# The row that one-hots are compared with, laid out as 15 padded runs of 32 (relational graph layer, one core)

## The chip, the core and the metric

The kernel runs on one core of one Trainium2 chip. The metric is the device time of one execution in microseconds, the median of several runs. A core has a matrix engine (PE), a vector engine (DVE), a scalar engine (ACT), GpSimd (POOL), a synchronisation engine (SP) and 16 DMA engines. Each engine works off its own queue in order, and engines meet at semaphores. "PEld" in the profile is the loading of matrix weights, and "POOLq", "SPq" and the like are the sequencers of the engines.

## The reference

There are 6250 nodes with 128 features each (`x`), and 106250 edges sorted by destination `dst`, each with a source `src` and one of 40 types. For each destination node and type the source rows are summed; each sum goes through the matrix of its type; the results, the counts of edges times a feature row per type, a norm by degree, a loop matrix, a ReLU, a residual and a layer norm follow.

```python
seg = edge_dst * 40 + edge_type
S = segment_sum(h[edge_src], seg, 6250 * 40).reshape(n, r, d)
cnt = segment_sum(ones, seg, 6250 * 40).reshape(n, r)
agg = einsum('nrd,rdf->nf', S, relation_weights) + cnt @ rFeatures
h = agg * deg ** -0.5
h = relu(h + h @ loop_weight)
x = layernorm(x + h)
```

## The kernel before

**Tiles.** The edges are cut into tiles of 128 (`P`), 831 of them (`USED`), 17 to a block (`TPB`); there are 49 blocks (`BLOCKS`), one for each 128 destination nodes. The edges of a tile fall on at most 12 neighbouring nodes (`WIN`), so a tile's sums fit a window of 40 types by 12 nodes, 480 columns.

**One tile.** GpSimd gathers the 128 source rows into `rows` (function `gather`, line 442: an indirect DMA from the DRAM table `x_parts`, in which each row of `x` lies as a rounded part and a rest, 1 KB together). DVE builds the one-hot matrix `hot` of 128 edges by 480 columns (`one_hot`, line 727): it compares a row of the numbers 0 to 479 (`iota`, FP16) with each edge's key `key_f`, type times 12 plus the node's place in the window, one number per partition. PE multiplies the 2 parts of the rows by `hot` into one of 7 PSUM banks (line 929, N = 480, twice for a tile), after a small product of 12 columns for the counts (line 922). ACT copies 11 of every 12 columns of the bank into `ring` (line 529), DVE adds the first column, which two tiles can share (line 829). `ring` holds the sums of four blocks.

**One block.** Once a block's tiles are in `ring`, PE multiplies the 41 pieces by the relation weights into `agg_ps` (line 939, spread over the tiles of the two next blocks), and DVE merges the 12 columns that spill into the next block (line 787), clears two stretches (lines 798 and 799, copies of `zeros`), builds two small one-hots for each half block (lines 736 and 739), and runs nine short steps of the norm (lines 750 to 779, among them the TENSOR_SCALARs of lines 758, 768 and 779).

**What sets the order.** Every engine's program is written out by hand. In DVE's step for tile t the one-hot of tile t + 7 (`AHEAD`; `hot` has 8 buffers) stands ahead of the add of tile t, which waits for ACT's copy of tile t. PE starts a pair of tiles t, t + 1 when DVE has added tile t - 6 (that frees the bank of tile t + 1). GpSimd issues the gather of tile t when PE has done tile t - 17 (`tile_done`; `rows` has 17 places).

**The first five blocks** (85 tiles, `PLAIN`) gather from `x` itself into `raw` (line 448), and ACT and DVE split these rows into the two parts (lines 505 and 723), while SP, ACT and DVE write the table `x_parts` in ten stages (lines 383, 498, 716 and 405). The gather of tile 85, the first of line 442, waits for the table, and for tile 68 to be done.

Of the kernel before, what the change touches and what calls it, by code (L numbers as in the profile page):

```python
# [5 lines left out]
ALU = mybir.AluOpType  # L6
# [3 lines left out]
FP16 = mybir.dt.float16  # L10
# [3 lines left out]
P = 128  # L14
N, E, D, R = 6250, 106250, 128, 40
# [12 lines left out]
WIN = 12  # L28
# [3 lines left out]
AHEAD = 7  # L32
COLS_T = TILES + TPB
POS = 20
POS_LOAD = 4
ROUND_SHIFT = 10
ROUND_MULT = -(-(1 << ROUND_SHIFT) // SEGS)
# [74 lines left out]
def build(nc, x, src_main, src_rest, dst_main, dst_rest, type_main, type_rest, r_features, relation_w, loop_w, out):  # L112
    with ExitStack() as ctx:
        x_parts = nc.dram_tensor("x_parts", [N, PARTS * D], F32, kind="Internal").ap()

        def sb(name, shape, dt):
            return ctx.enter_context(nc.sbuf_tensor(name, shape, dt))
# [4 lines left out]
        def sem(name):  # L122
            return ctx.enter_context(nc.semaphore(name))
# [9 lines left out]
        key_f = sb("key_f", [P, COLS_T], F32)  # L133
        pos = sb("pos", [1, BLOCKS * POS], I32)
        iota = sb("iota", [P, R * WIN], FP16)


        ring = sb("ring", [P, COLS, SEGS * SEG], F32)
# [9 lines left out]
        def pieces_in(flat):  # L148
# [8 lines left out]
        head, head_next, head_seg, head_off, head_gap, blk_i, rounds, pos_2d = (  # L157
            piece(POS)[0:BLOCKS].bitcast(I32) for _ in range(8))
        after = piece(TILES)
        iota_i = piece(R * WIN).bitcast(I32)  # L160
# [18 lines left out]
        hot = sb("hot", [P, HOTS, R * WIN], F32R)  # L179
# [77 lines left out]
        hot_ready = sem("hot_ready")  # L257
# [34 lines left out]
        def clear_ring(copy, segs):  # L292

            for s in segs:
                copy(ring[:, :, s * SEG:s * SEG + WIN], zeros[:])
                ins = copy(ring[:, :, s * SEG + BLOCK:(s + 1) * SEG], zeros[:])
            ins.then_inc(ring_zero, 1)
# [28 lines left out]
        def window(eng, regs, i, k):  # L326

            if k % POS_LOAD == 0:
                n = min(POS_LOAD, TPB - k)
                at = i * POS + k  # L330
                eng.load(regs[k:k + n], pos[0:1, at:at + n] if isinstance(i, int) else pos[0:1, bass.ds(at, n)])
# [20 lines left out]
        def column(t):  # L352
            return slice(t, t + 1) if isinstance(t, int) else bass.ds(t, 1)
# [15 lines left out]
        def _(sp):  # L369
# [20 lines left out]
            sp.wait_ge(pos_done, 1)  # L390
            sp.dma_start(pos[:].rearrange("o (b k) -> o b k", k=POS)[:, :, 0:TPB], pos_2d[:, 0:TPB]).then_inc(pos_ready, 16)
            w_v = relation_w.rearrange("r d f -> d r f")
# [23 lines left out]
        def _(pool):  # L416
# [8 lines left out]
            nc.gpsimd.iota(iota_i, pattern=[[1, R * WIN]], base=0, channel_multiplier=0)  # L425
            nc.gpsimd.iota(blk_i, pattern=[[0, POS]], base=0, channel_multiplier=1).then_inc(iota_done, 1)
            pool.wait_ge(const_done, 1)
# [216 lines left out]
        def _(dve):  # L644
# [9 lines left out]
            nc.vector.memset(hot_type[:, :, R:], 0.0).then_inc(types_padded, 1)  # L654
            dve.wait_ge(iota_done, 1)
            nc.vector.tensor_copy(iota[:], iota_i)
            dve.wait_ge(zeros_done, 1)
            clear_ring(nc.vector.tensor_copy, CLEARS[0])

# [64 lines left out]

            def one_hot(t, buffer):

                nc.vector.tensor_scalar(hot[:, buffer], iota[:], key_f[:, column(t)], None, ALU.is_equal).then_inc(  # L727
                    hot_ready, 1)

            def one_hot_types(i, h):  # L730

# [69 lines left out]
            def step(i, tiles, sums, late, fin):  # L801
                c = i - 3
                for k in range(TPB):
                    if sums and known(i, 2) and k == SAFE:
                        merge(i, tiles)
                    if tiles and k < tiles_of(i):
                        t = i * TPB + k
                        if k % 2 == 0:
                            ahead, j = pair_ahead(i, k, LOW_AHEAD)
                            if isinstance(ahead, int) and ahead < PLAIN_BLOCKS:  # L810
                                low(ahead, j)
                        if k == 4:
                            one_hot_types(i, 1)
                        if k == 14 and known_less(i, LAST):
                            clear(i)
                        if k == 13 and known_less(i, LAST):
                            one_hot_types(i + 1, 0)
                        if known_less(t + AHEAD, USED):
                            one_hot(t + AHEAD, (t + AHEAD) % HOTS)
                        if isinstance(i, int) and k in STAGE_AT.get(i, ()):  # L820
                            stage_low_part(stage_of(i, k))
                        start = window(dve, regs, i, k)

                        dve.wait_ge(copied, t + 1)
                        at_least(dve, added, t)
                        if k == 0 and known(i, 1):
                            dve.wait_ge(cleared, i)
                        a = ring[:, :, bass.ds(start, 1)]
                        nc.vector.tensor_tensor(a, a, win_ps[bank_of(t)][:, :, 0:1], ALU.add).then_inc(added, 1)  # L829
                    if fin:  # L830
                        finish(c, k)
# [9 lines left out]
            def in_order():  # L841
                one_hot_types(0, 0)
                for t in range(AHEAD):
                    one_hot(t, t % HOTS)
                for n in range(STAGED_FIRST):
                    stage_low_part(n)
                for j in range(LOW_AHEAD):
                    low(0, j)
                dve.wait_ge(pos_ready, 16)
                dve.wait_ge(ring_zero, len(CLEARS))  # L850
                run(dve, step)
                drain()
# [234 lines left out]
```

## Time and profile before

| | us |
|---|---|
| median of 3 runs | 1139.66 (1138.44 to 1141.38) |
| the profiled execution, its own time | 1136.47 |
| its span, first to last instruction | 1134.7 |

| engine | busy us | share of the span |
|---|---|---|
| PE | 978.5 | 86% |
| PEld | 863.6 | 76% |
| POOL | 822.3 | 72% |
| DVE | 749.0 | 66% |
| ACT | 525.5 | 46% |

Busy time is an average over stages that have different limits; what bounds a stage is read from which wait ends last in it. Records of DVE instructions overlap by up to 0.1 us, so that the busy time of an engine is less than the sum of its instructions' durations. A timeline row gives the start, the duration, the engine, the line of the code, what is written and read, and in brackets how long the engine had been idle and what released it.

### The profile page before, as it was taken

What the parts mean: (1) busy time and instruction counts of PE and PEld (TensorE: products, weight loads), DVE (VectorE), ACT (ScalarE), POOL (GpSimd) and SP (SyncE); (2) the same over time, 40 slices, a digit from 0 to 9 for tenths busy, and PEclk for the clock granted to TensorE, in tenths of its full rate; (3) what the DMA queues carried; (4) which work ended last, traced back from release to release, by engine and by line L of the source; (5) the groups of instructions that cost most, each with busy time, mean ns of one, the idle gap of its engine ahead of it and who ended that gap; (6) DMA issues with size and microseconds to landing.
All of it is one profiled execution on the core that took longest, in us unless ns stands there. A gap on an engine that the chain in (4) does not pass through costs nothing.

```text
span 1134.7 us, 25029 instructions
## 1 busy us (share of the span) xinstructions
PE 978.5 (86%) x6713; PEld 863.6 (76%) x6713; DVE 749.0 (66%) x2585; ACT 525.5 (46%) x1134; POOL 822.3 (72%) x846
## 2 busy tenths in 40 slices
PE   2345999998999999989899999989989999998997
PEld 1224999987887787888788878778878878877887
DVE  6344887777666666767766766666666666666663
ACT  2234765544444444445444444444444444444441
POOL 7773467777777777777777777777777777777770
PEclk9556999999999999999999999999999999999999
DMA  6543133333333333333333333333333333333330
GB/s 163 177 162 140 41 87 106 106 110 111 111 108 110 110 108 110 110 108 112 106 110 108 114 111 106 111 111 107 111 109 108 109 109 110 108 110 107 111 108 28
DMA packets 61567, 124.92 MB, mean 110 GB/s; under 512 B 15540, under 2 KB 33338, under 8 KB 61422
## 3 DMA queue, kind: packets, MB, share of 16 engines
q0 software_dynamic: 38512, 103.28, 31.6%
q1 hardware_dynamic: 8878, 13.65, 3.5%
q10 hardware_dynamic: 14032, 6.35, 2.0%
q8 instruction: 55, 0.90, 0.3%
q14 instruction: 90, 0.74, 0.2%
HBM read 113.62 MB, written 9.60 MB: 109 GB/s over the span
## 4 chain that ended last, share of the span: by engine, by line
PE 43%; DMA 33%; POOL 14%; issue 6%; DVE 2%; SPq 1%; ACT 1%; POOLq 0%; ACTq 0%; DVEq 0%
DMA rows<-x_parts,src 27%; PE win_ps L929 22%; PE agg_ps L939 18%; POOL rows L442 14%; DMA x_in<-x 6%; PE win_ps L1016 1%; PE win_ps L965 1%; DVE x_out L716 1%; ACT x_out L498 1%; PE win_ps L922 1%; SPq L397 0%; DMA w<-type_rest 0%; PE win_ps L902 0%; PE win_ps L964 0%; POOLq L441 0%
## 5 line engine op out<-in xcount | busy, mean ns | idle before, releaser
L442 POOL DMA_INDIRECT rows<-x_parts,src x746 | 734.5, 985 | 243.7 <-issue 121.9
L529 ACT COPY ring<-win_ps 128x451 f32 x831 | 464.3, 559 | 515.3 <-PE win_ps L929 503.0
L929 PE MATMUL win_ps<-hot,rows 128*128 128x480 f32 x1662 | 580.0, 434 | 83.8 <-DMA rows<-x_parts,src 71.8
L939 PEld LDWEIGHTS agg_ps<-ring,w 128*128 128x128 f32 x3936 | 553.5, 191 | 48.0 <-DVE ring L829 6.7
L939 PE MATMUL agg_ps<-ring,w 128*128 128x128 f32 x3936 | 561.8, 275 | 6.1 <-DVE ring L829 6.1
L727 DVE TENSOR_SCALAR hot<-iota,key_f 128x480 fp32r<-128x480 f16 x831 | 401.5, 484 | 0.3 <-issue 0.2
L829 DVE TENSOR_TENSOR ring<-ring,win_ps 128x41 f32 x831 | 188.4, 227 | 311.7 <-ACT ring L529 307.4
L929 PEld LDWEIGHTS win_ps<-hot,rows 128*128 128x128 f32 x1662 | 258.5, 194 | 138.9 <-DMA rows<-x_parts,src 124.9
L922 PEld LDWEIGHTS win_ps<-hot_node,hot_type 128*128 128x128 bf16 x831 | 81.6, 100 | 58.5 <-DVE hot_type L739 29.6
L922 PE MATMUL win_ps<-hot_node,hot_type 128*128 128x12 bf16 x831 | 85.8, 170 | 45.7 <-DVE hot_type L739 24.7
L448 POOL DMA_INDIRECT raw<-x,src x85 | 86.0, 1011 | 42.0 <-issue 22.6
L739 DVE TENSOR_TENSOR hot_type<-iota,typ_f 128x320 bf16<-128x320 f16 x98 | 49.5, 506 | 0.1
L716 DVE TENSOR_TENSOR x_out<-x_in,x_out 125x640 fp32r<-125x640 f32 x10 | 8.2, 824 | 50.0 <-ACT x_out L498 50.0
L498 ACT CAST x_out<-x_in 125x640 fp32r<-125x640 f32 x10 | 7.2, 724 | 67.9 <-DMA x_in<-x 54.6
L787 DVE TENSOR_TENSOR ring<-ring 128x492 f32<-128x492 f32 x48 | 31.7, 661 | 0.0
L799 DVE COPY ring<-zeros 128x492 f32<-128x492 f32 x48 | 31.4, 654 | 0.0
L798 DVE COPY ring<-zeros 128x492 f32<-128x492 f32 x48 | 31.0, 646 | 0.0
L736 DVE TENSOR_TENSOR hot_node<-iota,rel_f 128x96 bf16<-128x96 f16 x98 | 25.1, 256 | 0.4 <-issue 0.4
L965 PE MATMUL win_ps<-loop,agg_sb 128*128 128x128 f32 x96 | 22.4, 316 | 0.0
L964 PEld LDWEIGHTS win_ps<-ones,cnt_sb 128*128 128x128 f32 x96 | 18.0, 188 | 2.8
L505 ACT CAST rows<-raw 128x256 fp32r<-128x256 f32 (+1 forms) x45 | 17.5, 394 | 1.3 <-DVE out_sb L779 1.2
L723 DVE TENSOR_TENSOR rows<-raw,rows 128x256 fp32r<-128x256 f32 (+1 forms) x45 | 17.9, 403 | 0.2 <-ACT rows L505 0.2
(85 smaller groups left out, 247.2 us busy)
## 6 DMA issues: line engine op xcount, KB each, us to landing
rows<-x_parts,src POOLq DMA_INDIRECT x746
x_parts<-x_out SPq DMA_DIRECT2D x10, 625.0 KB
x_in<-x SPq DMA_DIRECT2D x10, 312.5 KB
out<-out_sb ACTq DMA_DIRECT2D x48, 64.0 KB
x_blk<-x ACTq DMA_DIRECT2D x47, 64.0 KB
w<-relation_w SPq DMA_DIRECT2D x8, 320.0 KB
raw<-x,src POOLq DMA_INDIRECT x85
w<-dst_main SPq DMA_DIRECT2D x1, 415.0 KB
```

The lines of the kernel that those rows point to most:

```text
L442: pool.indirect_dma_start(rows[0:n, k].rearrange("p c d -> p (c d)").bitcast(F32), None, x_parts, bass.IndirectOffsetOnAxis(ap=src[0:n, t: ...
L448: pool.indirect_dma_start(raw[:, t % RAW], None, x, bass.IndirectOffsetOnAxis(ap=src[:, t:t + 1], axis=0)).then_inc(gathered[k], 16)
L529: nc.scalar.copy(ring[:, :, bass.ds(start + 1, WIN - 1)], win_ps[bank_of(t)][:, :, 1:WIN]).then_inc(copied, 1)
L727: nc.vector.tensor_scalar(hot[:, buffer], iota[:], key_f[:, column(t)], None, ALU.is_equal).then_inc(hot_ready, 1)
L739: nc.vector.tensor_tensor(hot_type[:, at, 0:R], iota[:, 0:R].unsqueeze(1).to_broadcast([P, n, R]), typ_f[:, ts].unsqueeze(2).to_broadcast( ...
L787: nc.vector.tensor_tensor(ring[:, :, bass.ds(head, WIN)], ring[:, :, bass.ds(head, WIN)], ring[:, :, bass.ds(tail + BLOCK, WIN)], ALU.add) ...
L799: nc.vector.tensor_copy(ring[:, :, bass.ds(old + BLOCK, WIN)], zeros[:]).then_inc(cleared, 1)
L829: nc.vector.tensor_tensor(a, a, win_ps[bank_of(t)][:, :, 0:1], ALU.add).then_inc(added, 1)
L922: nc.tensor.matmul(banks[bank_of(n)][:, R * WIN:COLS * WIN], hot_type[:, n % TPB], hot_node[:, n % TPB], start=True, stop=True)
L929: ins = nc.tensor.matmul(banks[bank_of(t)][:, 0:R * WIN], rows[:, k, part, :], hot[:, t % HOTS], start=False, stop=(part == PARTS - 1), sk ...
L939: ins = nc.tensor.matmul(agg_ps[:], w[:, r, :], ring[:, r, bass.ds(seg, BLOCK)], start=(r == 0), stop=(r == COLS - 1))
L965: nc.tensor.matmul(ps[:, 0:D], agg_sb[:], loop[:], start=True, stop=True).then_inc(fin_done, 1)
```

## The change

A second row of the numbers 0 to 479, `iota_rows`, is made once at the start: 15 runs of 32 numbers with one pad element behind each, so that a run begins every 33 elements. The one-hot of a tile reads this row in place of `iota`. The numbers compared, the key, the result and its place are the same. `iota` stays, for the small one-hots.

```diff
+HOT_ROWS = 15
+HOT_RUN = R * WIN // HOT_ROWS
+assert HOT_ROWS % 2 and HOT_ROWS * HOT_RUN == R * WIN
...
         iota = sb("iota", [P, R * WIN], FP16)
+        iota_rows = sb("iota_rows", [P, HOT_ROWS, HOT_RUN + 1], FP16)
...
             nc.vector.tensor_copy(iota[:], iota_i)
+            nc.vector.tensor_copy(iota_rows[:, :, 0:HOT_RUN], iota_i.rearrange("p (a b) -> p a b", a=HOT_ROWS))
...
             def one_hot(t, buffer):
 
-                nc.vector.tensor_scalar(hot[:, buffer], iota[:], key_f[:, column(t)], None, ALU.is_equal).then_inc(
-                    hot_ready, 1)
+                nc.vector.tensor_scalar(hot[:, buffer].rearrange("p (a b) -> p a b", a=HOT_ROWS), iota_rows[:, :, 0:HOT_RUN],
+                                        key_f[:, column(t)], None, ALU.is_equal).then_inc(hot_ready, 1)
```

In the built program the order of DVE's instructions is the same but for one more cast. These are its rows at the start of the program, before; each names the line, the operation, what is written and read, and the form that is written (`w` is the buffer in which the whole numbers lie at that time; lines 295 and 296 clear `ring`):

```order
L656 CAST iota<-w 128x480
L295 COPY ring<-zeros 128x41x12
L296 COPY ring<-zeros 128x41x12
L661 CAST typ_f<-w 128x850
L662 CAST dst_f<-w 128x850
```

And now (the lines of the code stand four or five further down):

```order
L660 CAST iota<-w 128x480
L661 CAST iota_rows<-w 128x15x32
L299 COPY ring<-zeros 128x41x12
L300 COPY ring<-zeros 128x41x12
L666 CAST typ_f<-w 128x850
L667 CAST dst_f<-w 128x850
```

The cast into `iota_rows` is new and writes 15 runs of 32; nothing else moved. Further on DVE, where the tiles begin, the rows before are:

```order
L739 TENSOR_TENSOR hot_type<-iota,typ_f 128x8x40
L727 TENSOR_SCALAR hot<-iota,key_f 128x480 x7
L716 TENSOR_TENSOR x_out<-x_in,x_out 125x5x128
L723 TENSOR_TENSOR rows<-raw,rows 128x2x128 x4
L727 TENSOR_SCALAR hot<-iota,key_f 128x480
```

And now:

```order
L744 TENSOR_TENSOR hot_type<-iota,typ_f 128x8x40
L732 TENSOR_SCALAR hot<-iota_rows,key_f 128x480 x7
L721 TENSOR_TENSOR x_out<-x_in,x_out 125x5x128
L728 TENSOR_TENSOR rows<-raw,rows 128x2x128 x4
L732 TENSOR_SCALAR hot<-iota_rows,key_f 128x480
```

The one-hots stand where they stood. They read `iota_rows`, and the written form is still one run of 480: the program merges the 15 runs of `hot`, which touch, while those of `iota_rows` do not touch and stay apart.

## Rows read from the trace of the kernel before

**Rows 1.** The page: the chain that ended last, by engine.

```profile
PE 43%; DMA 33%; POOL 14%; issue 6%; DVE 2%; SPq 1%; ACT 1%; POOLq 0%; ACTq 0%; DVEq 0%
```

**Rows 2.** Timeline, POOL: start us, us, instruction, idle time and releaser.

```profile
147.09 0.97 POOL L442 DMA_INDIRECT rows<-x_parts,src  x1 [16.76 <-PE win_ps L929]
...
154.89 0.95 POOL L442 DMA_INDIRECT rows<-x_parts,src  x1 [0.30 <-issue]
...
1107.64 0.89 POOL L442 DMA_INDIRECT rows<-x_parts,src  x1 [0.30 <-issue]
```

**Rows 3.** Line 442 by itself: count, duration ns min/median/max, first and last start.

```profile
L442 POOL DMA_INDIRECT rows<-x_parts,src x746: 887/946/1357, 147.1 to 1107.6; - x187
```

**Rows 4.** The page, costliest groups: count, busy us, mean ns, idle before.

```profile
L442 POOL DMA_INDIRECT rows<-x_parts,src x746 | 734.5, 985 | 243.7 <-issue 121.9
...
L727 DVE TENSOR_SCALAR hot<-iota,key_f 128x480 fp32r<-128x480 f16 x831 | 401.5, 484 | 0.3 <-issue 0.2
L829 DVE TENSOR_TENSOR ring<-ring,win_ps 128x41 f32 x831 | 188.4, 227 | 311.7 <-ACT ring L529 307.4
```

**Rows 5.** Two stretches: busy us (count) of PE, PEld, DVE, ACT, POOL; clock, DMA.

```profile
108.00:147.00 39.00, 38.68 (x280) 36.23 (x281) 35.49 (x121) 28.61 (x66) 17.45 (x17) 0.96 0.17 52
...
228.00:1107.00 879.00, 798.52 (x5519) 705.35 (x5518) 591.05 (x2050) 414.71 (x886) 670.76 (x684) 1.00 0.38 109
```

**Rows 6.** These and the one between, DVE's one-hots of line 727 alone.

```profile
108.00:147.00 39.00, 17.41 (x37) 0.96 0.17 52
147.00:228.00 81.00, 36.22 (x76) 1.00 0.37 106
228.00:1107.00 879.00, 330.77 (x681) 1.00 0.38 109
```

**Rows 7.** Single lines of DVE: count, duration ns min/median/max, first and last start.

```profile
L727 DVE TENSOR_SCALAR hot<-iota,key_f x831: 448/464/702, 20.1 to 1103.0; 128x480 fp32r<-128x480 f16 x167
...
L758 DVE TENSOR_SCALAR h_sb<-fin_sb,norm x48: 274/277/515, 137.9 to 1121.7; 128x128 f32<-128x128 f32 x48
...
L787 DVE TENSOR_TENSOR ring<-ring x48: 656/660/672, 121.0 to 1112.5; 128x492 f32<-128x492 f32 x48
...
L799 DVE COPY ring<-zeros x48: 645/654/661, 67.0 to 1090.6; 128x492 f32<-128x492 f32 x48
```

**Rows 8.** Groups of DVE, each shape apart: count, busy us, mean ns.

```profile
L762 DVE TENSOR_TENSOR y_sb<-h_sb,x_blk 128x128 f32<-128x128 f32 x49 | 13.8, 282 | 0.1
```

**Rows 9.** Timeline of POOL beside DVE, at three places.

```profile
362.36 1.13 POOL L442 DMA_INDIRECT rows<-x_parts,src  x1 [0.30 <-issue]
362.59 0.46 DVE L727 TENSOR_SCALAR hot<-iota,key_f 128x480 fp32r<-128x480 f16 x1
...
367.69 0.95 POOL L442 DMA_INDIRECT rows<-x_parts,src  x1 [0.30 <-issue]
367.94 0.66 DVE L799 COPY ring<-zeros 128x492 f32<-128x492 f32 x1
...
498.96 0.95 POOL L442 DMA_INDIRECT rows<-x_parts,src  x1 [0.30 <-PE win_ps L929]
499.49 0.65 DVE L727 TENSOR_SCALAR hot<-iota,key_f 128x480 fp32r<-128x480 f16 x1
```

**Rows 10.** Timeline of DVE (adds of tiles 29 and 62, early work) and of SP.

```profile
107.48 0.22 DVE L829 TENSOR_TENSOR ring<-ring,win_ps 128x41 f32 x1
...
141.79 0.22 DVE L829 TENSOR_TENSOR ring<-ring,win_ps 128x41 f32 x1
...
6.22 0.71 DVE L661 CAST typ_f<-w 128x850 f32<-128x850 int32 x1 [2.42 <-DMA w<-type_rest]
...
22.80 0.82 DVE L716 TENSOR_TENSOR x_out<-x_in,x_out 125x640 fp32r<-125x640 f32 x1
...
27.87 0.43 SPq L383 DMA_DIRECT2D x_in<-x  x1
```

**Rows 11.** Timeline of PE: the start of the pair of tiles 68 and 69.

```profile
145.55 0.20 PE L922 MATMUL win_ps<-hot_node,hot_type 128*128 128x12 bf16 x2
```

## The prediction

> **What bounds the kernel now.** I read the page first, then the timeline of each engine. The page alone misleads: PE is busy for 86% of the span and POOL for 72% (the table above), and the chain that ended last is mostly PE and DMA [rows 1]. But POOL never waits in the long stage. The first gather of line 442 starts at 147.09 us, after a real wait of 16.76 us, and the last at 1107.64 [rows 2]. In between each of the 745 steps is one gather and then about 0.30 us idle, whichever releaser stands beside that idle time (the page has "issue" and PE); the pause is the same everywhere, so it belongs to the gather. The check: a gather takes 985 ns in the mean [rows 4], and (1107.64 - 147.09) / 745 = 1289 ns, so the pause is 304 ns. POOL is saturated for 960 us though it counts as busy for three quarters of them.
>
> The others have room. From 228 to 1107 us, 681 tiles pass at 1291 ns each. DVE works 591.05 / 681 = 868 ns for a tile [rows 5, 6]. PE was busy for 798.52 / 681 = 1173 ns of each; from 147 to 228 us, where its rows lie ready, it did 76 tiles in 81 us, 1066 ns for each, at a granted clock of 1.00 as later on (2.4 GHz) [rows 6]. The 16 DMA engines are busy for 38% [rows 5]. So there are three stages: up to 108 us the table is written, whose loads and stores alternate; to about 228 us PE is the bound, with its rows gathered ahead; from there POOL is, and it has been falling behind since its start at 147.09. The end is POOL's start, plus 746 gathers, plus a tail of 27.1 us behind the start of the last one (1134.7 - 1107.64).
>
> **Why a gather takes longer than it must.** Its median is 946 ns and its mean 985 [rows 3, 4]: most take 946, a part much longer, up to 1357. I laid the start of each gather beside DVE's instructions. 281 gathers have no one-hot running between 150 and 620 ns after their start (the first at 154.89, the last at 1107.64 [rows 2]); they take 945 ns in the mean and 963 at most. The other 465 take 1008. One pair shows it: a one-hot that starts 0.23 us after the gather makes it 1.13 us [rows 9]. It goes the other way too: where the gather is already in the middle of its work the one-hot pays, with 0.65 us in place of 0.46 [rows 9], and its maximum is 702 ns [rows 7]. And it isn't DVE as such: a longer copy of line 799 starts 0.25 us after the gather, and the gather still takes 0.95 [rows 9]. Line 787 and line 799 never leave 645 to 672 ns, while line 758 goes from 277 to 515 [rows 7].
>
> What sets the two kinds apart can be read from durations. Line 758 and the one-hot are both TENSOR_SCALARs with a number per partition: 128 elements in 277 ns, 480 in 464 [rows 7]; the slope is 187 / 352 = 0.53 ns for an element, the fixed part 209 ns. Lines 762 and 787 are both TENSOR_TENSORs: 128 elements in 282 ns [rows 8], 492 in 660 [rows 7]; the slope is 378 / 364 = 1.04 ns. So the one-hot goes at two elements in the time of one, and the kind that goes at double speed is the kind that excludes GpSimd. The copy of line 799 is the useful neighbour: it has one input like a one-hot, but its source is one run of 492 and its target 41 runs of 12. It takes 654 ns, the slow speed. A source and a target with unlike counts of runs, one even and one odd, lose the double speed here. The changed one-hot mirrors that: source 15 runs, target one run of 480.
>
> **The change, part by part.** *The one-hot itself.* At the slow speed it costs 209 + 480 x 1.04 = 709 ns. Bounds: 464 ns at the lower end, if nothing switches; at the upper end line 829, which steps by a whole row for each of its 41 elements and takes 227 ns [rows 4], so with the 149 ns that line 762 has beyond 128 x 1.04 that is (227 - 149) / 41 = 1.9 ns for an element, and a one-hot of 209 + 480 x 1.9 = 1121 ns. I take 709: the source still runs in pieces of 32 neighbours, like line 799's pieces of 12, which cost nothing extra. DVE then spends 709 - 484 = 225 ns more on each tile, 868 + 225 = 1093 ns, below POOL's 1250 and within the kernel's period. Cover: DVE waits for ACT before its adds; the one-hots stand seven tiles ahead, so what they add falls into these waits. It would be gone at 1250 ns.
>
> *The gather.* No long gathers are left: 945 + 304 = 1249 ns in place of 1289. The gain is the term that counts: 745 x 40 = 29.8 us by the starts; by the durations (985 - 946) x 746 = 29.1. I take 29.1. The short TENSOR_SCALARs of lines 758, 768 and 779 keep the fast form, about 132 of them in the stage. Of gathers without a one-hot in their middle, 14 had line 758 there, and none was over 948 ns; so I cost them at zero. Upper bound: as much as a one-hot costs now, 39 ns each, 5 us.
>
> *The start of the gathers.* It hangs on tile 68, and so on PE between 108 and 147 us. There DVE is the fuller engine than later: 35.49 of 39 us for 37 tiles [rows 5, 6], as it also splits raw rows. PE's pair 68, 69 needs DVE's add of tile 62. Before, DVE went from the add of tile 29 to that of tile 62, 33 steps, in 141.79 - 107.48 = 34.3 us [rows 10], 3.3 of them idle (of the 3.5 that the stretch has). Now 34.3 - 3.3 + 33 x 0.245 = 39.1 (against this stage's undisturbed 464 ns); with one longer one-hot ahead of tile 29's add, it is done at 107.48 + 0.25 + 39.1 + 0.2 = 147.0. PE began that pair at 145.55 [rows 11]. So the first gather starts some 1.5 us later. Behind it DVE needs about 1.2 us for a tile until the split rows end at tile 84, still under 1249, and POOL doesn't wait again. Bounds: nothing, if DVE's idle time was more than I counted; 5 us, if all of 35.49 + 37 x 0.245 - 39 = 5.6 shows.
>
> *The rest.* The added cast, about half a microsecond, lies ahead of the cast of line 661, before which DVE had stood idle for 2.42 us on a load [rows 10]: free; without that cover, 0.5 us. The seven one-hots ahead of the table's first part (line 716) are 1.7 us longer, but DVE was done with that part at 23.6 us and SP only came to the table's next load at 27.9, behind its weight loads [rows 10]: free. In the tail no one-hot is left (the last starts at 1103.0 [rows 7]).
>
> **Sum.** The span: 1134.7 - 29.1 + 1.5 = 1107.1. The profiled execution took 1136.47, 1.8 beyond its span, and the median of the runs shown is 3.2 above that. I carry the difference of 27.6 to the median: 1139.66 - 27.6 = 1112.1 us.
>
> **The rivals.** *Nothing switches.* If the engine keeps two elements at a time, the one-hot takes 464 ns, or 8 rows of 32 at 0.53 x 2 each, 480; the long gathers stay, and the time is 1140. Line 799 speaks against it, but there the odd count is the target's. The Trainium skill, VectorE: DVE Perf Modes, section on Mode 2×_2P, asks for outermost counts in source and destination that are both even, or odd and equal. By that rule one run of 480 gives the slow speed, and 15 runs on both sides would have given this rival; by the built program it is the first, so that the rule comes out at 1112, and line 799 agrees.
>
> *Half the gain.* The switch comes, but a run that begins at an odd element costs something, or the short TENSOR_SCALARs now meet the gathers. Each 0.1 us on a one-hot delays the first gather by 33 x 0.1 = 3.3 us; at 800 ns that is 3 us, with the 5 us of the short ones 8: 1120.
>
> *DVE becomes the bound (slower).* The place is DVE's queue from 228 us on: with a one-hot of H ns it needs 868 + H - 484 for a tile. From H = 866 on that is over POOL's 1250; from 905 on, over today's 1289. At the upper bound, 1121 ns, it is 1505 ns: 746 x 0.216 = 161 us more, with the delayed start some 1315 us. Against it: it takes 1.45 ns for an element, and the rows with runs of neighbours show 1.04 [rows 7, 8]. The Trainium skill, Vector Engine (DVE) Microarchitecture Reference, section 5.2, has one source that hops at every element at 1.73 ns and pairs that begin on an odd word at 1.30 (4-byte words). By its figures, an estimate, the one-hot would be 209 + 480 x 1.30 = 833 ns, still faster than before; only hops at every element would decide for this rival, and here there are 14 hops in 480. No row here shows an odd begin.
>
> **How the numbers follow.** Forecast, 1108 to 1117: 0.72. Half the gain, 1117 to 1130: 0.13. Nothing switches, 1138 to 1142: 0.10. DVE the bound, above 1143: 0.05. About 0.3% is what a measurement of this kernel can tell from no change, 3.4 us. So faster 0.85, same 0.10, slower 0.05. The range takes the forecast's case and the better part of the second: from 1107.5 (a gain of 29.8, no delay, and 2 us of scatter between medians) to 1122.
>
> **What would show it.** The one-hot at 700 to 720 ns with hardly any spread; the gathers of line 442 with a mean within 3 ns of their median of 946; starts 1250 ns apart; the first one at 148 to 149 us; DVE busy for 82 to 87% of the span, its waits for ACT nearly halved; lines 758, 768 and 779 still going up to 0.5 us. Wrong would be: one-hots at 460 to 480 (nothing switched); one-hots near 700 but a mean gather still at 985 (the exclusion has another cause than the speed); a first gather past 152 us (the early stage mis-sized); PE waiting for the one-hots after 228 us (DVE is the bound).

## The result and the profile after

| | before | after |
|---|---|---|
| median, us | 1139.99 (1138.44 to 1141.38, 4 runs) | 1123.00 (1122.10 to 1124.12, 4 runs) |
| ratio | | 0.985 (0.983 to 0.987) |
| span of the profiled execution, us | 1134.7 | 1120.2 |

The change gains 1.5%. The forecast was 1112.1 us with a range up to 1122: the direction was right, the gain was 17 us where 27.6 were expected, and the time lies just above the range. The two profiled executions are 14.5 us apart in span and not 17, since the one before lay 3.5 us below its median and the one after 0.9 below its own.

The page of the changed kernel, its busy time, the chain by engine, and the groups that answer to [rows 4] (one-hot now line 732, gather 446, add 834):

```profile
PE 972.0 (87%) x6713; PEld 861.6 (77%) x6713; DVE 914.3 (82%) x2586; ACT 525.7 (47%) x1134; POOL 806.2 (72%) x846
...
PE 46%; DMA 34%; POOL 9%; issue 6%; DVE 3%; ACT 1%; SPq 1%; DVEq 0%; POOLq 0%; ACTq 0%
...
L446 POOL DMA_INDIRECT rows<-x_parts,src x746 | 719.5, 964 | 245.0 <-PE win_ps L934 139.9
...
L732 DVE TENSOR_SCALAR hot<-iota_rows,key_f 128x480 fp32r<-128x480 f16 x831 | 585.2, 705 | 0.2
...
L834 DVE TENSOR_TENSOR ring<-ring,win_ps 128x41 f32 x831 | 186.7, 225 | 141.5 <-ACT ring L533 135.8
```

Each line by itself (count, duration ns min/median/max), to be read against [rows 3, 7]:

```profile
L732 DVE TENSOR_SCALAR hot<-iota_rows,key_f x831: 691/705/737, 20.4 to 1088.3; 128x480 fp32r<-128x480 f16 x167
```

```profile
L446 POOL DMA_INDIRECT rows<-x_parts,src x746: 942/946/1463, 147.4 to 1092.8; - x187
```

And the timeline of POOL, first and last gather, the counterpart of [rows 2]:

```profile
147.43 0.94 POOL L446 DMA_INDIRECT rows<-x_parts,src  x1 [18.08 <-PE win_ps L934]
...
1092.84 1.04 POOL L446 DMA_INDIRECT rows<-x_parts,src  x1 [0.31 <-issue]
```

The one-hot takes 705 ns, with a spread of 46 ns where it was 254: it went over to one element at a time (709 was worked out for that), and it is no longer stretched beyond 737. POOL is still the bound, its gathers back to back from 147.43 to 1092.84 us. The stream of 745 steps is 945.4 us where it was 960.6. That is 15.1 us less; the start (0.3 us later) and the tail (27.4 us for 27.1) give back 0.6, and the span is 14.5 us shorter. But a gather still takes 964 ns in the mean with a median of 946. The long gathers are fewer, not gone, and the longest is longer than before.

### The profile page after: what moved, and what is told of

Same layout as the page of the kernel before. It is cut to its first block, busy times and chain, and to the rows that moved or that the text cites. A ratio compares the mean times of both kernels' runs of the same rounds, so it can differ in the third digit from the quotient of the medians.

```text
span 1120.2 us, 25030 instructions
## 1 busy us (share of the span) xinstructions
PE 972.0 (87%) x6713; PEld 861.6 (77%) x6713; DVE 914.3 (82%) x2586; ACT 525.7 (47%) x1134; POOL 806.2 (72%) x846
## 4 chain that ended last, share of the span: by engine, by line
PE 46%; DMA 34%; POOL 9%; issue 6%; DVE 3%; ACT 1%; SPq 1%; DVEq 0%; POOLq 0%; ACTq 0%
DMA rows<-x_parts,src 28%; PE win_ps L934 24%; PE agg_ps L944 19%; POOL rows L446 9%; DMA x_in<-x 5%; PE win_ps L1021 1%; PE win_ps L970 1%; PE win_ps L927 1%; DVE x_out L721 1%; SPq L401 1%; ACT x_out L502 0%; DVE hot L732 0%; ACT ring L533 0%; DVE ring L834 0%; DMA w<-type_rest 0%
## 5 line engine op out<-in xcount | busy, mean ns | idle before, releaser
L446 POOL DMA_INDIRECT rows<-x_parts,src x746 | 719.5, 964 | 245.0 <-PE win_ps L934 139.9
L732 DVE TENSOR_SCALAR hot<-iota_rows,key_f 128x480 fp32r<-128x480 f16 x831 | 585.2, 705 | 0.2
L927 PE MATMUL win_ps<-hot_node,hot_type 128*128 128x12 bf16 x831 | 85.8, 170 | 43.8 <-DVE hot_type L744 22.4
L970 PE MATMUL win_ps<-loop,agg_sb 128*128 128x128 f32 x96 | 22.4, 316 | 0.0
```

What stands on the lines that cost most here:

```text
L446: pool.indirect_dma_start(rows[0:n, k].rearrange("p c d -> p (c d)").bitcast(F32), None, x_parts, bass.IndirectOffsetOnAxis(ap=src[0:n, t: ...
L732: nc.vector.tensor_scalar(hot[:, buffer].rearrange("p (a b) -> p a b", a=HOT_ROWS), iota_rows[:, :, 0:HOT_RUN], key_f[:, column(t)], None, ...
L927: nc.tensor.matmul(banks[bank_of(n)][:, R * WIN:COLS * WIN], hot_type[:, n % TPB], hot_node[:, n % TPB], start=True, stop=True)
L970: nc.tensor.matmul(ps[:, 0:D], agg_sb[:], loop[:], start=True, stop=True).then_inc(fin_done, 1)
```

## What holds the long gathers

I took all 746 gathers of the changed kernel against DVE's instructions again. 92 take more than 955 ns. In 83 of them, with 13.7 of the 14.1 us that all have beyond 946 ns, the gather ends 817 ns, to within 20, behind the end of an instruction that reads two inputs from SBUF and, but for three of them, was running when the gather began: the merge of line 792 (24 gathers, 6.6 us), the small one-hots of lines 744 and 741 (42, 5.5 us), and lines 767, 776 and 728 (17, 1.6 us). The timeline of POOL and DVE, a gather held and one not held:

```profile
154.92 0.54 DVE L744 TENSOR_TENSOR hot_type<-iota,typ_f 128x360 bf16<-128x360 f16 x1
154.95 1.33 POOL L446 DMA_INDIRECT rows<-x_parts,src  x1 [0.30 <-PE win_ps L934]
155.36 0.72 DVE L732 TENSOR_SCALAR hot<-iota_rows,key_f 128x480 fp32r<-128x480 f16 x1
...
1026.75 0.95 POOL L446 DMA_INDIRECT rows<-x_parts,src  x1 [0.30 <-PE win_ps L934]
1026.79 0.67 DVE L792 TENSOR_TENSOR ring<-ring 128x492 f32<-128x492 f32 x1
```

Line 744 ends at 155.46, and 155.46 + 0.82 = 156.28 is the end of the gather (154.95 + 1.33). The merge that starts 0.04 us behind its gather doesn't hold it. So a gather needs something at its start that a two-input instruction has taken; an instruction that ends within 946 - 817 = 129 ns of the gather's start costs it nothing. A two-input instruction that begins by itself later in the gather doesn't hold it.

With this in hand, the pair of [rows 9] reads otherwise than I read it. One more row of the kernel before, the instruction ahead of that one-hot, with the two rows again in mind:

```profile
362.01 0.66 DVE L787 TENSOR_TENSOR ring<-ring 128x492 f32<-128x492 f32 x1
```

The merge ends at 362.67; 362.67 + 0.82 = 363.49 is the end of that gather (362.36 + 1.13). The one-hot that I blamed only stood behind the merge.

The fast one-hot does hold gathers, but at two points, and not anywhere in their middle as I had it. Two pairs of the kernel before:

```profile
169.01 0.46 DVE L727 TENSOR_SCALAR hot<-iota,key_f 128x480 fp32r<-128x480 f16 x1
169.22 1.07 POOL L442 DMA_INDIRECT rows<-x_parts,src  x1 [0.30 <-PE win_ps L929]
...
171.85 1.03 POOL L442 DMA_INDIRECT rows<-x_parts,src  x1 [0.30 <-issue]
172.31 0.45 DVE L727 TENSOR_SCALAR hot<-iota,key_f 128x480 fp32r<-128x480 f16 x1
```

The first one-hot is running when its gather begins, and the gather ends 0.82 us behind the one-hot's end (169.47 + 0.82 = 170.29), as behind a two-input instruction. The second begins 0.46 us after its gather, and the gather ends 0.12 us behind the one-hot's end (172.76 + 0.12 = 172.88). Of the 212 gathers over 955 ns of the kernel before, with 29.0 us beyond 946, 106 are of the first kind (16.6 us) and 37 of the second (3.7 us; lags of 116 to 122 ns, one-hots that began 0.38 to 0.63 us after the gather). Another 65 (8.6 us) end 817 ns, to within 20, behind a two-input instruction. Four are left, with under 0.1 us. Where a one-hot began 0.13 to 0.35 us after the gather and nothing at double speed or with two inputs was running at its start (53 gathers), none took over 955 ns. In the changed kernel none of the second kind is left.

The Trainium skill, SBUF — State Buffer, section "Who interferes with whom", says that a DVE instruction with two SBUF inputs contends with a GpSimd instruction that reads SBUF, and one in a two-port mode with GpSimd at large. The trace agrees with both, with the 817 ns above; that a gather reads its row numbers (`src`) from SBUF at its start would fit the first, but no run here shows what it is that the gather needs, nor what it needs the second time.

## The experiments

Each has its gathers' row from the page; the medians are from the line's own view. Mean less median, times 746, is the sum that the long gathers cost; by this measure the kernel before has (985 - 946) x 746 = 29.1 us [rows 3, 4], the changed one 13.4. Each such sum comes from one trace. The kernel before ran beside all of them: 1140.31 us beside e1 to e4 (16 runs), 1140.95 beside e9 to e11 (9 runs).

**e1: an even count of runs.**

```diff
-HOT_ROWS = 15
+HOT_ROWS = 16
```

> The changed kernel with 16 padded runs of 30 in place of 15 of 32; all else is the same. Theory (what decides the one-hot's speed is that the counts of runs of source and target are unlike, one of them odd, and not the pad or the gaps): with 16 runs against one run of 480 both counts are even, the one-hot falls back to about 464 ns at the shortest, with a maximum near 700, and the time to that of the kernel before, 1136 to 1142 us. Rival (a source in padded runs is slow in itself): the one-hot stays at 705 ns and the time at 1123.

1140.29 us, ratio 1.000 (0.998 to 1.002). The one-hot and the gathers:

```profile
L732 DVE TENSOR_SCALAR hot<-iota_rows,key_f x831: 448/462/703, 20.3 to 1109.1; 128x480 fp32r<-128x480 f16 x167
```

```profile
L446 POOL DMA_INDIRECT rows<-x_parts,src x746 | 740.0, 992 | 244.6 <-issue 126.2
```

```profile
L446 POOL DMA_INDIRECT rows<-x_parts,src x746: 942/949/1372, 147.7 to 1113.8; - x187
```

With 16 padded runs the one-hot is fast again, and the whole gain is gone. Pad, gaps and odd begins (16 runs of 30 every 31 elements have them too) cost nothing. What decides is the count of the source's runs, 15 or 16, against a target in one run of 480 elements: the odd count is slow, the even one fast.

This trace has the fast one-hot and the two-input instructions of the kernel before, and its long gathers sum to (992 - 949) x 746 = 32.1 us where that one's sum to 29.1. By holder the difference is larger: 76 gathers with 13.1 us behind two-input instructions (65 with 8.6 there), 156 with 19.9 us behind the one-hot (143 with 20.3). So how much each kind holds differs by some us from one trace to the next, with the same work.

**e2 and e3: more load on DVE, with two inputs and with one.** e2 writes the larger small one-hot once more, e3 copies `zeros` twice more, both into the idle staging buffer.

```diff
+                if i >= 3:
...
+                    nc.vector.tensor_tensor(
+                        spare[:, 0:n * R].rearrange("p (t r) -> p t r", r=R),
+                        iota[0:X_PARTS, 0:R].unsqueeze(1).to_broadcast([X_PARTS, n, R]),
+                        typ_f[0:X_PARTS, ts].unsqueeze(2).to_broadcast([X_PARTS, n, R]), ALU.is_equal).then_inc(extra_done, 1)
```

```diff
+                if i >= 3:
+                    for _ in range(2):
...
+                        nc.vector.tensor_copy(spare[:, 0:COLS * (WIN + 1)].rearrange("p (r n) -> p r n", r=COLS)[:, :, 0:WIN],
+                                              zeros[0:X_PARTS]).then_inc(extra_done, 1)
```

> The changed kernel, and from block 3 on DVE makes the second small one-hot (two inputs in SBUF, 320 or 360 elements, 0.5 us) a second time into a spare buffer, 92 more such instructions. Theory (a gather whose start falls into a DVE instruction with two SBUF inputs waits for its end and then needs about 817 ns): such stretches are longer by 0.44 us twice a block, the sum of what gathers take beyond 946 ns goes from 14.3 us to 25 to 32, and the time from 1123 to 1134 to 1141 us. Rival (the gathers that are still long in the changed kernel come from DVE being busier, or from DMA): 92 x 0.44 = 40 us more of DVE's time in 960 would add 0 to 3 us.

> The changed kernel, and from block 3 on two more copies of zeros (one input, the slow form, 492 elements, 0.65 us) behind the two clears, into a spare buffer, 90 more instructions, some 52 us more of DVE's time: more load than in the run with the small one-hots made twice. Theory (only two SBUF inputs, or the double speed, keep a gather waiting): gathers stay at a mean of 963 to 966 ns, the time stays within 2 us of 1123. Rival (DVE's load makes gathers long): the mean rises to 975 or more, the time by 8 us or more.

e2: 1131.44 us (1130.81 to 1134.03), e3: 1126.82 (1126.18 to 1128.67). The page's gathers of e2, then of e3:

```profile
L447 POOL DMA_INDIRECT rows<-x_parts,src x746 | 728.4, 976 | 245.7 <-PE win_ps L945 137.1
```

```profile
L447 POOL DMA_INDIRECT rows<-x_parts,src x746 | 723.7, 970 | 246.4 <-PE win_ps L944 140.0
```

The order is as expected, the sizes are not: e2 added 8.4 us to the changed kernel's 1123 for 33 us more of DVE's busy time where 11 to 18 were expected, e3 3.8 for 46 us where under 2 were. Both have a median gather of 949 ns and not 946, which is 2.2 us in each; e1 and e10 have it too, and its cause is open. Beyond it e2 has (976 - 949) x 746 = 20.1 us and e3 15.7, against 13.4. So the added two-input instructions cost about three times what the one-input ones cost (6.7 and 2.3 us), with more of DVE's time in the cheaper run. In e3 it is line 747, the small one-hot, that holds more gathers than before (43 with 8.0 us, by the same 817 ns; line 744 of the changed kernel has 37 with 5.2). That the added copies shifted it against the gathers is a guess; the copies themselves held none.

**e4: the merge as a copy.**

```diff
-                nc.vector.tensor_tensor(
-                    ring[:, :, bass.ds(head, WIN)], ring[:, :, bass.ds(head, WIN)],
-                    ring[:, :, bass.ds(tail + BLOCK, WIN)], ALU.add).then_inc(merged, 1)
+                nc.vector.tensor_copy(ring[:, :, bass.ds(head, WIN)], zeros[:]).then_inc(merged, 1)
```

> The changed kernel with the merge (492 elements, two inputs in the ring, 0.66 us) replaced by a copy of zeros of the same size and duration to the same place; this leaves out the sums that cross two blocks. Theory: the merges' share of the long gathers goes, 6.7 of 14.3 us by the trace of the changed kernel, and the time falls from 1123 to 1115 to 1118 us. Rival (the one-hot that follows the merge is what makes the gather long): the copy is followed by the same one-hot, nothing changes, 1123.

1117.04 us (1115.27 to 1118.77), as the theory has it:

```profile
L446 POOL DMA_INDIRECT rows<-x_parts,src x746 | 712.2, 955 | 245.0 <-PE win_ps L932 138.7
```

**e9 and e10: without two-input instructions, behind the slow and the fast one-hot.** The merge as in e4, and from block 3 on:

```diff
+                if i >= 3:
+                    flat = zeros[:].rearrange("p r n -> p (r n)")
...
+                    nc.vector.tensor_copy(
+                        hot_node[:, at].rearrange("p t n -> p (t n)").rearrange("p (a b) -> p a b", a=runs),
+                        flat[:, 0:runs * (run + 1)].rearrange("p (a b) -> p a b", a=runs)[:, :, 0:run])
+                    ts_, cols = (5, 64) if n == 8 else (9, R)
+                    nc.vector.tensor_copy(
+                        hot_type[:, at.start:at.start + ts_, 0:cols],
+                        flat[:, 0:n * R].rearrange("p (a b) -> p a b", a=ts_)).then_inc(types_ready, 1)
+                    return
```

> The kernel of the run without the merge and the small one-hots again (both replaced by copies of zeros, sums across blocks and counts by type left out), for a time on a chip where the gathers are back to back: the last such run had gathers of 947 ns in the mean, but all its engines stopped together 168 times or so, and its time can't be used. Theory (two SBUF inputs at the start of a gather are all that is left): gathers at 947 to 953 ns, the stream of 746 at 934 to 938 us, the time 1109 to 1113 us, ratio to the kernel before 0.973 to 0.977. Rival (another cost of 8 us or more came with the slower one-hot): above 1116.

> The same two replacements in the kernel before, with its fast one-hot (sums across blocks and counts by type left out). Theory (each kind holds up its own gathers): the fast one-hots' share stays, 17 to 22 us of 29; the time is 7 to 12 us below the kernel before, 1128 to 1133. Then the one-hot's share is what the change took away. Rival of my prediction (the one-hots hold up all of the long gathers): no change, 1138 to 1141.

e9: 1111.38 us, ratio 0.975 (0.972 to 0.978). e10: 1130.87 us, ratio 0.991 (0.988 to 0.995). Line 446 of e9 and line 442 of e10, by themselves and on the page:

```profile
L446 POOL DMA_INDIRECT rows<-x_parts,src x746: 880/946/1136, 150.3 to 1083.3; - x187
...
L446 POOL DMA_INDIRECT rows<-x_parts,src x746 | 707.0, 948 | 245.1 <-PE win_ps L944 147.1
```

```profile
L442 POOL DMA_INDIRECT rows<-x_parts,src x746: 887/949/1241, 147.8 to 1104.1; - x187
...
L442 POOL DMA_INDIRECT rows<-x_parts,src x746 | 730.1, 979 | 244.6 <-issue 122.5
```

Both times and both ratios came out as the theories have them. The stream of e9, 1083.3 - 150.3 = 933.0 us, and the fast one-hots' share in e10, 22.4 us, lie just outside what was named (934 to 938, and 17 to 22). Together with the two kernels they make a square:

| long gathers, us (median time, us) | merge and small one-hots as they are | replaced |
|---|---|---|
| fast one-hot | 29.1 (1140.0) | 22.4 (1130.9) |
| slow one-hot | 13.4 (1123.0) | 1.5 (1111.4) |

By these four traces the two causes don't add up: the fast one-hot costs 15.7 us beside the others and 20.9 alone, the others 6.7 beside it and 11.9 alone. With e1's trace in the first cell (32.1 us) it is 18.7 and 20.9, 9.7 and 11.9; by the times it is 17.0 and 19.5, 9.1 and 11.6. That a gather which one cause no longer holds at its start can fall to the other is plausible, but a difference of 2 to 5 us between single traces doesn't show it. What the square shows is that each cause costs time without the other, and that both together are all but 1.5 us of the long gathers.

**e5 to e8: the same questions on another chip.** e5 is the changed kernel once more, e8 is e9's kernel. e7 makes the larger small one-hot in three pieces, in steps of their own; e6 makes the merge in three as well.

```diff
+                        if k == 1:
+                            types_nodes(i, 1)
+                        if k in (2, 3, 4):
+                            types_piece(i, 1, k - 2)
...
+                        if k == 9 and known_less(i, LAST):
+                            types_nodes(i + 1, 0)
+                        if k in (11, 12, 13) and known_less(i, LAST):
+                            types_piece(i + 1, 0, k - 11)
```

> The changed kernel as it is, on the chip of the three runs that follow, so that they can be compared with it there: 1121 to 1127 us by both theories, gathers with a median of 946 to 949 ns, beyond it 13 to 17 us in sum.

> The changed kernel with the same work in pieces: the larger of the small one-hots (360 and 320 elements) in three pieces of 2 or 3 tiles, the merge in three pieces of 13 or 14 relations, each piece in a step of its own with the one-hot of 480 behind it. Theory (a gather that starts inside an instruction with two SBUF inputs, or a chain of such, waits for its end and needs 817 ns from there; so what an instruction costs grows with the square of its length beyond 0.13 us, and a one-hot between two pieces lets the gather in): of the 12 us that merges and small one-hots cost, 2 to 4 stay; the sum of what gathers take beyond their median is 4 to 6 us, the time 8 to 10 us below the changed kernel on this chip, 1113 to 1117. Rival (the sum of such stretches decides, not their length, or the lock goes over to the one-hot that follows): the same 14 us or, with 6 more instructions a block, more; 1122 to 1128.

> Of the run in pieces the small one-hots alone; the merge stays whole. Theory: some 4 to 5 us below the changed kernel on this chip, 1117 to 1121, the merges' 6 to 7 us stay. Rival: no change, 1122 to 1126.

> The changed kernel with the merge and, from block 3 on, both small one-hots replaced by copies of zeros (one input, the slow form, the same number of elements); this leaves out the sums across blocks and the counts of edges by type. Theory: of the long gathers only those beside the norm's steps and the first blocks are left, 1 to 3 us, all gathers at a mean of 947 to 953 ns, and the time is 10 to 13 us below the changed kernel on this chip, 1110 to 1114, which is also what my forecast of 1112 had taken for the changed kernel itself. Rival (something else than two inputs makes them long): above 1118.

On this chip the kernel before took 1388.44 us (29 runs), and these 1396.05, 1402.06, 1394.32 and 1394.25, all far from the 1110 to 1128 us expected. The page of e5, its chain and its gathers:

```profile
PE 57%; another core or an unknown queue 14%; issue 13%; ACT 9%; DMA 3%; DVE 2%; ACTq 2%; SPq 0%; DVEq 0%
...
L446 POOL DMA_INDIRECT rows<-x_parts,src x746 | 719.2, 964 | 482.8 <-PE win_ps L934 202.8
```

The gathers were no longer than elsewhere (964 ns), but POOL stood idle for twice as long (482.8 us), 168 times for more than 0.4 us, and in the one stretch that I followed, at 405 us, PE, ACT and DVE stood idle with it; the granted clock was 0.87 over the whole execution where it was 0.97. What stopped them stays open. There POOL isn't the bound, and the change makes the kernel slower: ratio 1.005 (1.003 to 1.007). The times decide nothing about e6 to e8. Their gathers do: means of 960 (e6), 959 (e7) and 947 (e8) against 964, at a median of 946 in all. e8 is as the theory has it. The pieces saved only 3 to 4 us in gathers, where e6 was expected to save 8 to 10. The smallest one-hot, 0.25 us long, now held 31 gathers in e6 and 26 in e7, where it held 10 in e5. In 27 and 20 of them it stood right behind the norm's step with two inputs (line 786 of e6), where I had put it. Two in a row can hold a gather to the end of the second: of the gathers that began while the norm's step still had more than 135 ns to run, 13 of 14 in e6 and 6 of 7 in e7 were held so.

**e11: pieces that never stand two in a row.**

```diff
+            def behind_hot(i, k):
+                if k == SAFE and i >= 2:
+                    merge(i, True, 1)
+                if k == 0:
+                    types_nodes(i, 1)
+                if k in (1, 2, 3):
+                    types_piece(i, 1, k - 1)
+                if i < LAST:
+                    if k == 8:
+                        types_nodes(i + 1, 0)
+                    if k in (9, 11, 13):
+                        types_piece(i + 1, 0, (k - 9) // 2)
```

> The changed kernel, work and result the same: the larger small one-hots in pieces of 2 or 3 tiles and the merge in two halves, each piece alone between instructions that don't have two SBUF inputs (behind the big one-hot and ahead of the add of line 829's kind), so that no two of them stand in a row as they did in the run in pieces (the norm's line with two inputs, then the smallest one-hot). Theory (a gather waits for the end of the chain of such instructions that is running when it starts, so the square of a chain's length counts): of 14 us beyond the median 5 to 8 stay, the time is 1114 to 1118 us, ratio 0.977 to 0.981. Rival (pieces save nothing, and five more instructions a block cost): 1122 to 1127.

1116.71 us (1114.90 to 1118.70), ratio 0.980 (0.977 to 0.982): as the theory has it, and faster than both kernels, with the same work. (The changed kernel's 1122.10 to 1124.12 us were not taken beside it; its ratio to the kernel before is 0.983 to 0.987.) The page's gathers, and two of them beside what held them:

```profile
L447 POOL DMA_INDIRECT rows<-x_parts,src x746 | 712.6, 955 | 248.1 <-PE win_ps L975 137.6
```

```profile
700.86 0.28 DVE L786 TENSOR_TENSOR y_sb<-h_sb,x_blk 128x128 f32<-128x128 f32 x1
700.91 1.05 POOL L447 DMA_INDIRECT rows<-x_parts,src  x1 [0.30 <-issue]
...
702.20 0.40 DVE L819 TENSOR_TENSOR ring<-ring 128x240 f32<-128x240 f32 x1
702.27 1.15 POOL L447 DMA_INDIRECT rows<-x_parts,src  x1 [0.30 <-PE win_ps L975]
```

Half of the 13.4 us is left, (955 - 946) x 746 = 6.7. A short piece can still be met by a gather, but holds it only until the piece ends: 701.14 + 0.82 and 702.60 + 0.82 are the two ends to within 0.01 us.

## Why the prediction came out as it did

**The bound.** Right on the chips where the gathers run back to back: POOL is saturated from its first gather to its last, before and after, with the pause of 304 ns between them, which stayed. On the chip of e5 to e8 it isn't.

**The one-hot.** Right: 709 ns predicted, 705 measured, and the copy of zeros into 41 runs was the right neighbour. Where nothing switches (e1) the time is the one that this rival had, 1140.

**The gather.** This step failed, and all of the miss is in it. It said that "no long gathers are left" and counted 29.1 us; 15.7 went, and 13.4 stayed. The mechanism that it named was there: the fast one-hot and the gather do shut each other out, and no gather of the changed kernel is held by it to speak of. What was wrong is the share: of the 29 us, 20.3 stood behind one-hots and 8.6 behind two-input instructions, and in the changed kernel these hold 13.7 (in e1, with the fast one-hot, 13.1, so that part of the rise lies between traces). The place was wrong too: not a one-hot anywhere between 150 and 620 ns, but one that runs at the gather's start or begins some 0.4 us after it. I sorted the gathers by whether a one-hot ran in their middle, and found none long without one. But DVE's program has a one-hot behind nearly every merge and small one-hot, at once, so that the same sorting also caught the gathers that these had held: cause and companion came in the same window. The row of line 787 that "never leaves 645 to 672 ns" showed only that the merge is never held up itself; I read it as if it held nobody. Two rows more, what ran at the start of the gather and when it ended, would have shown the constant 817 ns behind the merge. The rest of the sum holds: e9, with the merge and nearly all of the small one-hots replaced, took 1111.4 us, and the forecast was 1112.1.

**The start of the gathers.** Right in mechanism and about right in size. DVE was the bound from 108 to 147 us, busy for 38.97 of 39 us where it had been 35.49 [rows 5]. The stretch, and the timeline of DVE in the changed kernel at the point where that stage begins:

```profile
108.00:147.00 39.00, 38.17 (x277) 35.21 (x276) 38.97 (x112) 26.91 (x63) 16.47 (x17) 0.97 0.16 48
...
106.86 0.48 DVE L744 TENSOR_TENSOR hot_type<-iota,typ_f 128x320 bf16<-128x320 f16 x1
```

In the kernel before the same instruction began at 107.79. From there to the first gather it was 39.3 us and now is 40.6, 1.3 more where 1.5 was predicted; that the first gather came only 0.3 later is because this stage began 0.9 earlier, for which I found no cause. So the first gather at 147.43, outside the 148 to 149 that was named, is partly luck of that execution: with the same slow one-hot it came at 149.1, 148.6, 148.6, 150.3 and 149.3 in e2, e3, e4, e9 and e11, and with the fast one at 147.7 and 147.8 in e1 and e10.

**What was costed at nothing** stayed nothing or nearly so: the added cast, the first one-hots, the tail (0.3 us). The short TENSOR_SCALARs held three gathers, with 0.2 us. DVE is busy for 82% of the span (82 to 87 predicted), and from 228 us on for 726.48 / 682 = 1065 ns a tile (1093 predicted), still under POOL's 945.4 / 745 = 1269:

```profile
228.00:1092.00 864.00, 791.80 (x5525) 704.47 (x5524) 726.48 (x2048) 415.02 (x886) 656.23 (x683) 1.00 0.39 111
```

**The rivals.** Half the gain is what came, at 1123 in its stretch of 1117 to 1130, but not by its mechanism: odd begins cost the one-hot nothing (e1, and 705 ns where 709 were worked out without them), and the short TENSOR_SCALARs have 0.2 us. DVE did not become the bound on chips where the gathers run back to back. The range was too narrow at its upper end because all 29 us had been given to one cause and no rival divided them.

## What to carry to other kernels

Where GpSimd issues gathers back to back and is the bound, a DVE instruction at double speed and one with two SBUF inputs can be a cost on GpSimd's path, though DVE has time to spare. Here it paid to make the frequent one slower on purpose (17 us), and the rare long ones short and never two in a row (6 us more). To find who holds whom, look at what runs when the held instruction starts and whether its end follows the holder's by a constant; a window in its middle also catches whatever always stands behind the real cause. And take such a gain only where that engine is the bound: on a chip where it wasn't, the same change cost 0.5%.

## What the runs showed of the hardware that was not expected

- A gather of 128 rows issued by GpSimd waits at its start for the end of a DVE instruction with two SBUF inputs, and then takes 817 ns more (814 to 824 in the changed kernel); unheld it takes 946. One that begins 0.04 us ahead of the merge isn't held; but line 776 held one that its record has 0.045 us behind, so the records don't give this edge more finely.
- A fast one-hot holds a gather in the same way at its start, and a second time: a gather during which it begins some 0.4 to 0.5 us in ends 119 ns behind it (37 gathers of the kernel before). Between these two points it holds none.
- Two instructions with two SBUF inputs in a row can hold a gather to the end of the second, but needn't: lines 741 and 744 of the changed kernel did so in one of six cases, lines 786 and 753 of e6 in 13 of 14. What decides stays open. In e2, where two small one-hots stood in a row behind the smallest, the longest gather took 1919 ns.
- The number of runs in the source alone switched a one-hot between 462 (16 runs) and 705 ns (15 runs), at the same count of elements.
- The same kernel took 1123 us on one chip and 1396 on another, with the same lengths of its gathers.
